# Two scratch halves in turn for the ternary weights of a convolution-and-FFN layer (8 cores, Trainium2)

## The reference

```python
x = x + conv(layernorm(x), w_lin)      # 16 heads, 31 taps, softmax over the taps
x = x + (layernorm(x) @ w_eff.T + bias)

def ternary_quantize(w):
    delta = 0.7 * mean(abs(w))
    return where(w > delta, 1.0, where(w < -delta, -1.0, 0.0))
w_eff = ternary_quantize(weight) * alpha      # weight is 1024 x 1024
```

## Time and profile before

| what | value |
|---|---|
| median of 2 runs | 410.32 us (408.65 to 411.99) |
| the profiled execution | 411.76 us |
| its span, slowest core (core 1) | 410.2 us |
| spans of the 8 cores | 394.1 to 410.2 us |
| mean granted TensorE clock of the cores | 0.690 to 0.718 of full speed |

### The profile page before, as it was taken

The page is one execution under the profiler, slowest core; times in us unless marked ns, Lnnn a source line. Parts: engine busy times, 40 slices in busy tenths (PEclk is TensorE's granted clock), DMA queues, the critical chain, the costliest instruction groups (busy, mean ns, idle before and its releaser), DMA issues.

```text
span 410.2 us, 2983 instructions; the slowest of 8 cores (394.1 to 410.2 us)
## 1 busy us (share of the span) xinstructions
PE 157.6 (38%) x940; PEld 91.8 (22%) x940; DVE 132.4 (32%) x250; ACT 71.2 (17%) x78; POOL 6.6 (2%) x9
## 2 busy tenths in 40 slices
PE   0000303500000160052009597138660059999990
PEld 0000001200000020021004597138660013333430
DVE  1363822393300033002303385508461003232321
ACT  0007057703210033011201100000004544000000
POOL 6000000000000000000000000000000000000000
PEclk9999999955555595568557755555555569999997
DMA  7999953004699945674650899999902677985322
GB/s 198 280 260 282 344 151 51 1 0 98 136 178 283 147 84 168 148 141 102 190 117 13 154 179 250 155 187 193 160 0 101 168 194 199 255 199 184 137 102 103
DMA packets 85560, 64.53 MB, mean 157 GB/s; under 512 B 69024, under 2 KB 70048, under 8 KB 85544
## 3 DMA queue, kind: packets, MB, share of 16 engines
q10 hardware_dynamic: 15216, 42.02, 36.5%
q1 hardware_dynamic: 68696, 19.21, 28.4%
q0 software_dynamic: 1632, 3.12, 3.4%
HBM read 23.14 MB, written 25.40 MB: 118 GB/s over the span
## 4 chain that ended last, share of the span: by engine, by line
DMA 31%; PE 23%; SPq 20%; DVE 10%; ACT 6%; issue 3%; DVEq 2%; ACTq 2%
DMA wTf<-wT 10%; SPq L199 9%; SPq L207 9%; DMA stage<-wpad 7%; DMA xn1d<-xn 6%; DMA wet<-stage 4%; PE ps_ff L659 4%; PE ps_wp L659 4%; PE ps_ff L661 4%; PE ps_wp L661 3%; PE ps_at L636 3%; PE ps_wp L609 3%; DMA xn1T<-xn1d 3%; SPq L221 2%; ACT wet L455 2%
## 5 line engine op out<-in xcount | busy, mean ns | idle before, releaser
L609 PE MATMUL ps_wp<-wlTb,xn1T 128*128 128x496 bf16 x64 | 22.1, 524 | 134.0 <-DMA xn1T<-xn1d 134.0
L636 PE MATMUL ps_at<-wins,wet 128*64 128x64 bf16 x512 | 50.8, 305 | 28.7 <-DMA wet<-stage 20.7
L636 PEld LDWEIGHTS ps_at<-wins,wet 128*64 128x64 bf16 x512 | 50.2, 216 | 29.6 <-issue 29.6
L350 DVE TENSOR_REDUCE sumc<-wpad 128x16 f32<-128x496 bf16 x16 | 10.7, 669 | 114.1 <-ACT wpad L473 113.9
L609 PEld LDWEIGHTS ps_wp<-wlTb,xn1T 128*128 128x128 bf16 x64 | 8.0, 129 | 147.7 <-issue 146.0
L659 PE MATMUL ps_ff<-wtern,xn2T 128*128 128x512 bf16 x64 | 25.3, 395 | 29.0 <-DMA xn2T<-xn2d 29.0
L360 DVE TENSOR_TENSOR xs<-ps_at,xs 128x1024 f32<-128x1024 f32 x16 | 19.6, 1222 | 28.1 <-PE ps_at L636 28.1
L137 DVE BATCH_NORM_STATS2 statsw<-xs 128x6 f32<-128x512 f32 x32 | 22.0, 687 | 15.3 <-DMA xs<-x 13.9
L564 ACT ACTIVATE xn2r<-xs,scn,scr 128x1024 bf16<-128x1024 f32 x16 | 18.6, 1230 | 39.6 <-DVEq L383 25.8
L661 PE MATMUL ps_ff<-wtern,xn2T 128*128 128x512 bf16 x64 | 25.2, 393 | 0.0
L659 PE MATMUL ps_wp<-wtern,xn2T 128*128 128x512 bf16 x64 | 24.3, 380 | 0.0
(11 more groups left out here) (87 smaller groups left out, 111.6 us busy)
## 6 DMA issues: line engine op xcount, KB each, us to landing
stage<-wpad ACTq DMA_DIRECT2D x16, 512.2 KB, 6.4
wins<-xn1d ACTq DMA_DIRECT2D x16, 512.0 KB, 12.8
out<-outst ACTq DMA_DIRECT2D x8, 1024.0 KB, 5.1
wTf<-wT ACTq DMA_DIRECT2D x1, 4096.0 KB, 40.3
xn2d<-xn2r ACTq DMA_DIRECT2D x4, 1024.0 KB, 5.1
xn1d<-xn ACTq DMA_DIRECT2D x3, 1024.0 KB, 5.9
xs<-x ACTq DMA_DIRECT2D x2, 1024.0 KB, 11.8
xs<-x SPq DMA_DIRECT2D x2, 1024.0 KB, 19.2
```

The costliest lines, as they stand in the source:

```text
L609: mm = tensor.matmul(pw[:, 0:F], xn1T[:, cc * T + i * 128:cc * T + (i + 1) * 128], wlTb[:, cc * F:(cc + 1) * F], start=(cc == 0), stop=(cc ...
L636: mm = tensor.matmul(pa[64 * jj:64 * jj + 64, h * R:(h + 1) * R], lhsT, rhs, start=True, stop=True)
```

## The change

The scratch gets a second half. Even passes use columns 0 to 1023 behind each of the two places, odd passes columns 1024 to 2047. ScalarE's wait is one pass looser: from pass 2 on it waits for `tern` to reach q - 1, and pass 1 has no wait. The number and the shapes of the computing instructions are as before; one wait is gone.

```diff
@@ VectorE
         for q in range(8):
             vector.wait_ge(sems["tch"], q + 1)
-            vector.tensor_tensor(wtern[:, q * C:(q + 1) * C], wet[:, 0:C],
-                                 wet[:, WET_ROWS_PAD:WET_ROWS_PAD + C], ALU.add).then_inc(sems["tern"], 1)
+            o_ = (q % 2) * C
+            vector.tensor_tensor(wtern[:, q * C:(q + 1) * C], wet[:, o_:o_ + C],
+                                 wet[:, WET_ROWS_PAD + o_:WET_ROWS_PAD + o_ + C],
+                                 ALU.add).then_inc(sems["tern"], 1)
@@ ScalarE
         for q in range(8):
-            if q > 0:
-                scalar.wait_ge(sems["tern"], q)
-            scalar.sign(wet[:, 0:C], wTf[:, q * C:(q + 1) * C], bias=cstb[:, 4:5])
-            scalar.sign(wet[:, WET_ROWS_PAD:WET_ROWS_PAD + C], wTf[:, q * C:(q + 1) * C],
+            if q > 1:
+                scalar.wait_ge(sems["tern"], q - 1)
+            o_ = (q % 2) * C
+            scalar.sign(wet[:, o_:o_ + C], wTf[:, q * C:(q + 1) * C], bias=cstb[:, 4:5])
+            scalar.sign(wet[:, WET_ROWS_PAD + o_:WET_ROWS_PAD + o_ + C], wTf[:, q * C:(q + 1) * C],
                         bias=cstb[:, 0:1]).then_inc(sems["tch"], 1)
```

## The result

| | median | runs | lowest to highest |
|---|---|---|---|
| before | 411.62 us | 10 | 408.65 to 418.71 |
| changed | 405.51 us | 11 | 401.69 to 414.70 |

The ratio is 0.9846, with a 95% interval of 0.9803 to 0.9890: 6.3 us less (0.0154 x 411.62), between 4.5 and 8.1. By the 2% mark that is no change; by its interval it is a gain. The profiled execution took 414.70 us, the longest of the eleven, so the end of its chain is not set beside the earlier trace rows.

A forecast was written before the change was run, and what follows sets the result against it. The prediction took a chain of steps waiting on each other, no engine busy over 38%, as the bound. The loop's 7.2 us (bounds 5.7 to 7.3) off the 410.32 us median gave 403.1 us, range 399.3 to 407.3.

The forecast's parts named there:

- The loop is on the path: Ternary loop: ScalarE's statistics wait, the writes of `stage` and `xn1d` and all up to the FFN hang on its end.
- A pass of two signs, 1.05 each, no wait left: Ternary loop: 16 signs run one behind the other, 1.05 us each, last sign 7.17 us earlier; pass 3.08 us before.
- The 0.34 us of the last pass: Extra gap before the loop's last pass: if it stays the gain is 6.8 us, if it vanishes 7.2; 7.2 taken.
- the prediction's second sum: Loop gain from the waits: ScalarE's seven waits for VectorE, 6.6 us, plus 0.7 of broken overlap, 7.3 us.
- The bound of 1.15 per sign: Lower bound in the loop: if additions stretch the signs, 1.15 us each without overlap, gain 5.7 us.
- A sign costs less than in pairs: Rival in the loop: a sign takes the skill pages' 946 ns, gain 8.7 us, time 401.6 us; chance 0.03.
- Nothing takes the place of the wait: Behind the loop: projection tile and loads are ready in time; ScalarE next stops at the statistics, same 10.9 us or so.
- The sum: Whole kernel: statistics, writes and transposes come 7.2 us earlier on every core; 410.32 - 7.2 = 403.1 us, 1.75% less.
- Half given back: Rival: some half of the gain lost in the aggregation stretch, the `xn1d` write or 1.15 us signs; 406.7 us, chance 0.08.
- ScalarE still waits: Rival in the loop: ScalarE waits on VectorE or for its own reasons, pass stays 3.08 us; 410.3 us, chance 0.02.
- A worse aggregation: Rival, `stage` transposes to last statistics: cores' transposes meet less luckily, costing 11.7 us; 414.8 us, chance 0.04.
- a luckier stretch: Rival, `stage` transposes to last statistics: that stretch gives another 4 us; 399.1 us, chance 0.07.

The follow-up runs named there:

- e1: Changed kernel's two scratch halves, but ScalarE waits for `tern` to reach q as before the change; ratio 1.0055 to the kernel before.
- e5: Changed kernel with one more ScalarE sign in every pass, written where nobody reads; ratio 1.0041 to the kernel before.
- e8: Repeat of e6 (changed kernel, passes 5 to 7 made by VectorE alone); 403.88 against 416.82 us before, ratio 0.9665.
- e3: Changed kernel with VectorE's statistics of tiles 8 to 15 moved into the loop, behind each addition; 402.19 against 419.63 us before, ratio 0.9615.
- e2: Changed kernel with four scratch parts instead of two, ScalarE waiting for `tern` to reach q - 3; ratio 0.9883 to the kernel before.
- e7: e3's kernel with ScalarE making four of the eight sums of |weight| that VectorE made; 399.31 against 416.82 us before, ratio 0.9531.
- e4: Kernel before, one scratch and its wait kept, with the statistics moved into the loop as in e3; 410.65 us, ratio 0.9723.
- e9: The changed kernel unaltered, timed a third time, on the chip of e7 and e8; 411.22 against 416.82 us before, ratio 0.9839.
- e6: Changed kernel with passes 5 to 7 made by VectorE alone (two comparisons and a subtraction); 407.54 us (4 runs) against 419.63 before, no interval.

## Why the prediction was right

*The loop is on the path.* Right. e1, e5, e8 and e3 move the same stretch by other amounts (0.0, -1.0, 13.6 and 15.6 us), and the end follows.

*A pass of two signs, 1.05 each, no wait left.* Right, 1.04 in the trace; e2 shows that no wait was hidden. The 0.34 us of the last pass, left open between 0 and 0.34, vanished. The gain of the loop is 7.32 against 7.17; the prediction's second sum, 7.3 from the waits, hit it. Additions beside signs don't stretch them: 1.13 with and without. The bound of 1.15 per sign, gain 5.7, is out.

*A sign costs less than in pairs* (gain 8.7): wrong. Sixteen signs in a row stay at 1.04. The Trainium skill's page Perfetto Trace Analysis (Optimizing Scalar/DVE Operations), with the rate per element of its page ScalarE: Activation LUTs (Step-by-step: what each stage is for), gives the prediction's estimate of 0.946 us. The trace of a sign disagrees by a tenth of a microsecond. That of e7's Abs, which reads no bias from a tile, does not: its readout starts 0.95 us behind it (last section). So the fixed part of the estimate fits this Abs and is too small for a sign, whose bias comes from the tile `cstb`.

*Nothing takes the place of the wait.* Right for this change, but with less room at one place than was said. The prediction had the first projection tile ready at 71.4 for an exponential at 73.4, from matmuls evenly spaced. In e8 and e7 ScalarE waits for this tile, and it gets it 3.67 us behind the tile's first matmul (73.58 - 69.91, 73.64 - 69.97), not 2.9. In the changed kernel, core 6, that is an estimated 71.66 for an exponential at 72.56: 0.9 us of room, not 2.0. The cover named, the wait for the statistics, is there in e8 (4.89 us left) and used up in e7 on most cores.

*The sum.* 403.1 us was forecast, 405.51 measured. Of the 2.4 between them 1.3 are the kernel before, which came to 411.62 with ten runs where two had given 410.32; 1.1 are the gain, 6.1 between the medians in place of 7.2. Whether that is noise or a little given back the runs don't settle: the measured gains of the same loop, 6.3, 6.0, 6.7 and 4.9 with e2, all lie under 7.3, with 7.3 in each interval. Weighted together they give an estimated 6.2 us, from 5.0 to 7.3, so that 7.3 is at the edge. By their ratios the four larger shifts (e4, e8, e3, e7) all lie over their distance, by their medians two of them do. One microsecond is below what can be told.

*The rivals.* Half given back is outside the intervals of the first measurement and of e9. That ScalarE still waits is refuted by the timeline: no sign of passes 1 to 7 has a wait. A worse aggregation and a luckier stretch were not tested by themselves; the rest of one microsecond leaves room for a small part of either, and none is needed for the forecast.

*What was less right.* The chance of 0.35 for a gain over 2% was generous in view of a sum of 1.75%; the range's lower end, 399.3, is not quite the lucky stretch that it is said to reach, 399.1. And the slowest core was taken from one profile: which core is slowest changed from profile to profile (core 1 before; cores 6, 4 and 2 in three of the changed kernel), so how near three cores end to each other in one execution says little of the next.

## What to carry to other kernels

Two engines that pass one scratch back and forth run in turns, and each waits while the other works; a second half lets the slower one run without a pause. First follow what comes behind the pair to the end: here the pair was on the path, as far as the times can tell for its whole length, though ScalarE was busy for 17% of the time only. Then ask for the idle time that is left: VectorE's 1.39 us per pass held work that stood behind the loop, and moving it there shortened the distance by 8.3 us, more than the second half's 7.3, until in e7 a third engine's result ended last.

## What the runs showed of the hardware that was not expected

A float32 comparison with a second operation on VectorE, 128 x 1024, starts 0.66 us behind the one before, while the sums of |weight| over the same input start 1.13 apart (42.5 to 50.4 for the eight of L314 before). ScalarE's Abs with an accumulated output goes at 1.04 us per 128 x 1024, as a plain sign does, with its readout of 0.19 us in that time: the readout starts 0.95 us behind the Abs, and the next Abs 0.09 behind the readout. Timeline of e7, core 4:

```profile
43.40 1.06 ACT L444 ACTIVATE wins<-wTf 128x1024 bf16<-128x1024 f32 x1 [2.08 <-DMA wTf<-wT]
...
44.36 0.19 ACT L444 ACTIVATION_READ_ACCUMULATOR wins<-wTf 128x1 f32 x1
44.45 1.04 ACT L444 ACTIVATE wins<-wTf 128x1024 bf16<-128x1024 f32 x1
```

The three kinds of ScalarE instruction over 128 x 1024 elements, float32 in and bf16 out, last 1.04 us (Abs, no tile operand beside the input), 1.13 (the sign, bias from a tile) and 1.23 (the normalisation, scale and bias from tiles). It looks as if each such operand costs 0.09 us; the functions differ as well, and that was not taken apart.

VectorE's or TensorE's work beside them changes the signs' 1.04 in none of the profiles shown. And the last pass of the loop has its 0.34 us gap wherever ScalarE has waited for VectorE in the loop (before, e1, e4), and not in the runs where it has not (the changed kernel, e2, e3, e5 to e8). The gap of 0.41 us in e6 and e8 stands elsewhere, behind a wait for TensorE and one for VectorE.
